# A graph layer and a mixture of experts on one core: nine chunks instead of eight, 33 stored blocks, and another listing of the accumulating transfers

## What is computed

```python
def gnn(features, src, dst, W, b):            # 6250 nodes, 106250 edges, 256 features
    xw = features @ W
    msg = xw[src] * rsqrt(max(out_degree, 1))[src][:, None]
    agg = segment_sum(msg, dst, 6250)
    return relu(agg * rsqrt(max(in_degree, 1))[:, None] + b)

def ffn(x):                                   # 8 experts, hidden width 1024, the 2 best for each row
    top_p, top_idx = top_k(softmax(x @ Wr + br), 2)
    weights = top_p / top_p.sum(-1)
    xe = layernorm(x) * ln_g[e] + ln_b[e]
    y[e] = gelu(xe @ W1[e] + b1[e]) @ W2[e] + b2[e]
    return weights[0] * y[top_idx[0]] + weights[1] * y[top_idx[1]]

x = x + gnn(layernorm(x), src, dst, W, b)
x = x + ffn(layernorm(x))
```

## Time and profile before

| | |
|---|---|
| device time, median of 3 runs (lowest, highest) | 1668.92 us (1660.3, 1669.75) |
| device time of the profiled execution | 1661.44 us |
| its span, first to last instruction | 1660.0 us |
| TensorE (PE) busy, weight loads (PEld) | 1192.6 us (72%), 989.6 us (60%) |
| VectorE (DVE), ScalarE (ACT), GpSimd (POOL) busy | 952.5 (57%), 595.0 (36%), 1116.0 us (67%) |
| mean granted TensorE clock | 0.82 |
| moved by DMA | 354.75 MB, mean 214 GB/s |

### The profile page before, as it was taken

One profiled execution on the slowest core, in us unless ns is written; L12 is line 12 of the kernel. 1 busy time (PEld: TensorE's weight loads), 2 busy tenths in 40 slices (PEclk: granted clock), 3 DMA queues, 4 the chain that ended last, 5 costly groups with the idle time before them and its releaser, 6 DMA issues.

```text
span 1660.0 us, 26618 instructions
## 1 busy us (share of the span) xinstructions
PE 1192.6 (72%) x9098; PEld 989.6 (60%) x9098; DVE 952.5 (57%) x2502; ACT 595.0 (36%) x1169; POOL 1116.0 (67%) x1115
## 2 busy tenths in 40 slices
PE   6954565647358645995599659969839858689995
PEld 5954344535146314982488439848728747479984
DVE  8997456656434353656264734764645749466552
ACT  4954011111032004440345025516315335356662
POOL 5006777777777777777777777777777757673333
PEclk9999566666578557996699769979959969799998
DMA  6027866675375447974787469759658578999882
GB/s 187 1 98 266 266 219 203 213 232 179 117 260 163 110 119 261 312 222 129 260 270 253 138 217 316 255 192 305 188 189 292 179 252 265 258 294 305 264 251 51
DMA packets 195546, 354.75 MB, mean 214 GB/s; under 512 B 25572, under 2 KB 93446, under 8 KB 195412
## 3 DMA queue, kind: packets, MB, share of 16 engines
q1 hardware_dynamic: 130120, 205.39, 36.6%
q0 software_dynamic: 58928, 141.26, 29.5%
q10 hardware_dynamic: 6364, 6.40, 1.2%
HBM read 290.80 MB, written 64.07 MB: 214 GB/s over the span
## 4 chain that ended last, share of the span: by engine, by line
PE 35%; DMA 25%; POOL 19%; issue 9%; DVE 8%; ACT 3%; SPq 0%; POOLq 0%; DVEq 0%; ACTq 0%
DMA gt<-zt,srcI 12%; POOL gt L832 9%; PE ps L1251 9%; PE ps L1266 9%; PE ps L1165 8%; DMA out<-gt,toks 6%; POOL xs L861 6%; DMA out<-acc 3%; PE ps L1140 2%; POOL out L891 2%; PE ps L1176 2%; DVE ohl L1340 2%; PE ps L1203 2%; DMA xb<-xs 1%; ACT h L1112 1%
## 5 line engine op out<-in xcount | busy, mean ns | idle before, releaser
L832 POOL DMA_INDIRECT gt<-zt,srcI x832 | 834.1, 1003 | 254.2 <-issue 181.6
L1165 PE MATMUL ps<-gt,S 128*128 128x257 f16 x1664 | 345.7, 331 | 200.3 <-DMA gt<-zt,srcI 198.9
L1165 PEld LDWEIGHTS ps<-gt,S 128*128 128x128 f16 x1664 | 203.5, 152 | 298.2 <-DMA gt<-zt,srcI 282.8
L1251 PE MATMUL ps<-xe,w1b 128*128 128x256 f16 x2688 | 343.2, 282 | 36.0 <-DVE xe L1656 18.9
L1266 PE MATMUL ps<-w2b,hT 128*128 128x256 f16 x2688 | 315.5, 275 | 13.5 <-DVE yb L1688 7.7
L1251 PEld LDWEIGHTS ps<-xe,w1b 128*128 128x128 f16 x2688 | 269.9, 101 | 78.6 <-DVE xe L1656 21.6
L1112 ACT ACTIVATE h<-ps,cb 128x256 f32<-128x256 f32 x448 | 227.1, 557 | 241.4 <-PE ps L1251 236.4
L1662 DVE SCALAR_TENSOR_TENSOR hT<-h,cb,hT 128x512 f16<-128x512 f32 x224 | 167.7, 750 | 237.4 <-ACT hT L1116 236.8
L1266 PEld LDWEIGHTS ps<-w2b,hT 128*128 128x128 f16 x2688 | 264.3, 99 | 47.5 <-issue 15.4
L1116 ACT ACTIVATE hT<-h,cb 128x512 f16<-128x512 f32 x224 | 161.7, 722 | 7.3
L1090 ACT ACTIVATE aT<-ps 128x256 f32<-128x256 f32 x98 | 37.4, 381 | 314.7 <-PE ps L1196 314.6
(11 more groups left out here) (264 smaller groups left out, 1246.7 us busy)
## 6 DMA issues: line engine op xcount, KB each, us to landing
w1b<-ws SPq DMA_DIRECT2D x56, 1024.0 KB, 6.5
w2b<-ws SPq DMA_DIRECT2D x56, 1024.0 KB, 8.1
ws<-w2b SPq DMA_DIRECT2D x16, 1024.0 KB, 5.0
xb<-xs SPq DMA_DIRECT2D x56, 260.0 KB, 8.3
gt<-zt,srcI POOLq DMA_INDIRECT x832, 4.2
ys<-yb SPq DMA_DIRECT2D x34, 256.0 KB, 7.8
w1b<-in_L_ffn_W SPq DMA_DIRECT2D x8, 1024.0 KB, 8.7
hT<-in_L_ffn_W SPq DMA_DIRECT2D x8, 1024.0 KB, 13.9
```

The source lines that it names most:

```text
L832: e.indirect_dma_start(out=gt[:, i % NG, :], out_offset=None, in_=zt, in_offset=bass.IndirectOffsetOnAxis(ap=srcI[:, c, r:r + 1].bitcast(u ...
L1165: inst = e.matmul(PS[r % 2][:, 0:257], S[:, r % NS, :, c], gt[:, i % NG, part * 257:part * 257 + 257], start=(c == 0 and part == 0), stop= ...
L1251: inst = e.matmul(UP[n % 2][:, z * BS:(z + 1) * BS], w[:, l, kk, j * 128:(j + 1) * 128], xe[m % 2][:, k, kk, :], start=(kk == 0 and l == 0 ...
```

## The change

`ENDS` gives nine chunks: the tiles behind 36 are cut at 40, 43, 46 and 49, not at 41, 45 and 49. The number of blocks in them goes from 5, 4, 18 to 4, 3, 3, 17. `EARLY` is counted from the end, so 33 blocks are stored and 23 given, and 40 tiles are fetched and combined. The sums go from three ranges (tiles 10 to 20, 20 to 30, 30 to 41) to two of 15 tiles. The groups behind tile 36 are complete after rows 86, 93, 99 and 104, where they were after 82, 89, 97 and 104.

In the planner a give or a sum is listed only when GpSimd will be free within 0.5 us, not 2.6; a give counts as 3.7 us of GpSimd and 4.5 until it has landed (3.4 and 5.0 before), a sum as 2.0 and 3.0 + 1.1 us a tile (1.3 us a tile of GpSimd and 5.0 before). A `cg` or `xs` step is listed only when GpSimd will be free within 0.3 us, and not when an accumulating transfer is waiting to be listed and the one before will have landed within the next microsecond; before, `cg` needed GpSimd free within 2.5 us and `xs` nothing. A `cc` comes 6 us behind its `cg` in the plan, not 2.

```diff
-ENDS = [10, 17, 24, 31, 36, 41, 45, 49]
+ENDS = [10, 17, 24, 31, 36, 40, 43, 46, 49]
...
-EARLY = LAST - 2
+EARLY = LAST - 3
...
-NSUM = -(-(TG - TP) // 11)
+NSUM = 2
...
     def step_give():
 
-        if max(s["chain"], s["plain"], s["base"]) > s["now"] or clock["POOL"] > s["now"] + 2.6:
+        if max(s["chain"], s["plain"], s["base"]) > s["now"] or clock["POOL"] > s["now"] + 0.5:
             return False
         if batches and batches[0][0] <= s["now"]:
             b = batches.popleft()[1]
-            emit("sums", b, (("POOL", 1.3 * (SUMS[b][1] - SUMS[b][0])),), s["now"])
+            emit("sums", b, (("POOL", 2.0),), s["now"])
+            s["chain"] = clock["POOL"] + 3.0 + 1.1 * (SUMS[b][1] - SUMS[b][0])
             s["summed"] += 1
         elif gives:
-            emit("give", gives.popleft(), (("POOL", 3.4),), s["now"])
+            emit("give", gives.popleft(), (("POOL", 3.7),), s["now"])
+            s["chain"] = clock["POOL"] + 4.5
             s["given"] += 1
         else:
             return False
-        s["chain"] = clock["POOL"] + 5.0
         return True
...
-                if kind == "cg" and clock["POOL"] > s["now"] + 2.5:
+                if kind in ("cg", "xs") and (clock["POOL"] > s["now"] + 0.3 or (gives or batches) and s["now"] + 1.0 < max(s["chain"], s["plain"], s["base"]) + 1.0 < s["now"] + 2.0):
                     continue
...
-                chain.at = end + 2.0 if kind == "cg" else s["now"] if kind == "xs" else end
+                chain.at = end + 6.0 if kind == "cg" else s["now"] if kind == "xs" else end
```

## The result

The changed kernel takes 1672.55 us (median of 8 runs, 1670.07 to 1674.4), the kernel before 1666.21 us in the runs beside it (8 runs, 1660.3 to 1670.04). The ratio is 1.0051, 95% interval 1.0035 to 1.0068: the change makes the kernel 0.5% slower, where 1641 us was forecast. In the profiled executions the span goes from 1660.0 to 1670.3 us.

What follows compares the result with a forecast made beforehand. No engine bounds the whole: first GpSimd's gathers, at the end the chain of accumulating transfers. First give 1390, plus 102.3 and 43, puts the twelfth give at 1535, the last at 1621, span 1631.7, median 1641; range 1624 to 1664.

Steps and rivals of the forecast that it cites:

- Fetch stage: GpSimd's gathers up to the last one: 43 tiles scattered before it, not 45, and first `cg` at 1338 to 1340.
- the 5.2 us: Before the last gather on GpSimd: 4 scatter DMAs of 1.30 us less, so it comes 5.2 us earlier.
- First give: First accumulating transfer after ten stored tiles: 1339 + 45.7 + 7.8, less stalls, taken as 1390, bounds 1385 and 1396.
- the old 45.7 us: Old time between first `cg` and first give, kept as base, with 7.8 us added for six scatters.
- Up to 4: Listing `cc` 6 us behind its `cg`, not 2, delays the tenth `cc` by up to 4 us.
- Sums: Two accumulating sums of 15 tiles in the chain: 21.5 us each, 43 together, bounds 29 and 48; three old ones took 47.3.
- the old 1.53 us a tile: Proportional cost of a sum from the old kernel: 1.53 x 15 = 22.9 us for fifteen tiles.
- Spacing of the gives: Gives while `cg` are still issued: two pairs behind each, 9.3 us apart, bounds 8.9 and 11.7, about 11 gives.
- the spacing stays: Rival: gives land late behind moving gathers, spacing near 11.7 us; span 1649, median 1658; chance 0.14.
- The last chunk and the late end: Last chunk's scatters at 1386, first `y` 1430, last 1606; final gives then at 5.5 us, last starting at 1621.
- The rival "slower": GpSimd runs behind its list, VectorE and TensorE wait, 5.9 us in each of 12 cycles; median 1693; chance 0.09.

Runs made afterwards that it cites:

- The chunks alone: Kernel before with the nine new chunks, old planner and three sums of ten tiles: 1675.43 us, ratio 1.0058.
- the planner's half alone: Changed kernel with the old chunks put back, new planner and two sums of 15 and 16 tiles kept: 1670.48 us, ratio 1.0022.
- the one-tile sum: Changed kernel with each of the two sums cut to its first tile, order of steps kept: 1657.66 us, ratio 0.9937.
- The loose listing: Changed kernel with only the conditions for listing a give, `cg` and scatter set back to the old ones: 1684.08 us, ratio 1.0112.
- The run that halved it by another order: Changed kernel with each `cc` gathered behind a sum listed only after that sum's planned landing: 1677.21 us, ratio 1.0061.

## Why the prediction was wrong, by its steps

The starts below are those of the forecast and of the changed kernel's trace.

| point | forecast | measured | lost up to here |
|---|---|---|---|
| first `cg` | 1339 | 1342.64 | 4 |
| last chunk's scatters | 1386 | 1391.77 | |
| first give | 1390 | 1413.47 | 23.5 |
| first give behind the last sum | 1498 | 1541.09 | 43.0 |
| last give | 1621 | 1660.45 | 39.5 |
| span | 1631.7 | 1670.3 | 38.6 |
| first, last `y` of the last chunk | 1430, 1606 | 1451.98, 1642.73 | 22, 36.7 |

The forecast did not say where the last sum stands. The fourth line is worked out from its terms for the seven gives that came before it: 1390 + 7 x 9.3 + 2 x 21.5 = 1498.1.

**Fetch stage, 4 us.** Before the last gather 43 tiles were scattered, as forecast, and the hole of 11.19 us in front of the first `cg` shrank to 4.48. But the four scatters fewer did not bring the 5.2 us: the last gather is issued at 1337.21, in the kernel before at 1336.81. The 832 gathers kept GpSimd busy 839.0 us, not 834.1; why is open.

**First give, 23.5 us: the failed step.** It was put as the old 45.7 us plus six scatters minus a few us of stalls. From the first `cg` to the first give it took 70.8 us (1342.64 to 1413.47), not 51. Its parts counted GpSimd's instructions, but the first give can't be issued before the tenth `cc` and its store, and that `cc` stands in VectorE's queue. The sentence "one routing more costs VectorE some 12 us of small instructions, in a stretch where it is busy 18.23 us of 40: nothing" took its cover from 1200:1240. In the stretch that mattered VectorE was already busy 44.53 us of 60 in the kernel before:

```profile
1340.00:1400.00 60.00, 50.52 (x390) 41.52 (x390) 44.53 (x142) 32.33 (x60) 38.15 (x38) 0.86 0.79 254
```

and is busy 47.91 of 60 after. That is only 3.4 us more, so the load alone doesn't explain 18 us: what matters is the order in the queue. The last chunk's routing, which came behind the tenth `cc`, now stands ahead of it. The tenth `cc` slips from 1383.34 to 1401.32. The chunks alone show it (1397.20), and listing it first gives 1385.51. The give then waits for a plain store too, 11.13 us in that run, for which the forecast had no term. And while the `cc` is late, the planner lists other work: 21 `cg` pairs and both chunks' twelve scatters go before the first give, where the forecast had 17 pairs and six scatters. It put the last chunk's scatters at 1386, ahead of its own first give, and had no term for them. "Up to 4" for the 6 us behind `cg` was small for the old chunks, where the planner's half alone delays the first give by 11.8 us.

**Sums, 9.0 us.** 26.75 + 25.23 = 52.0 us, not 43, outside the upper bound of 48, and more than the 45.9 that the old 1.53 us a tile make of 30 tiles. What was overlooked stands in the forecast's own rows: the DMA share was 1.02 from 1495 to 1510, so a sum's duration says what else was moving as much as what it moves itself. The runs bear that out: sums of ten tiles landed after 11.0 to 19.4 us, sums of fifteen after 18.2 to 27.5. There is a fixed part: one tile alone held the chain 8.23 us and each further tile added 1.2. By that line ten tiles would hold it 8.23 + 9 x 1.2 = 19.0 us; the last ten-tile sums with the new chunks held it 19.61 and 19.66, where the old kernel had 15.94 and 13.07. The first sum is another matter: with the 16 gathers listed behind it GpSimd was busy 23.0 us (21.8 with the one-tile sum), so with this list a shorter transfer could not bring it below that. The wrong step was to take durations of one stretch as those of another: the old kernel with two sums shows 21.82 and 25.76 us too, nothing less than its three.

The Trainium skill (DMA: Bandwidth & Descriptors, section on the anatomy of one DMA) gives 2.0 us plus bytes over 436 GB/s, by which 1.97 MB are an estimate of 6.5 us; the trace has 25.81 and 24.38. The measurement decides, and the formula holds here even less than for ten tiles.

**Spacing of the gives.** Four gives in front of the first sum take 36.99 us, where 4 x 9.3 = 37.2 was forecast: this step was right for these four, two pairs behind each give and no rival "the spacing stays". The loose listing shows 11.5 to 11.9 in its place. But there were seven gives in this phase and not eleven, since 21 pairs had gone ahead of the first give and not 17. And the three gives behind the first sum take 15.76, 11.55 and 11.34 us, 38.65 and not 27.9: 10.8 us. Behind a long sum the gathers and the give itself land late. The mean of 9.3 came from stretches with short sums.

The Trainium skill (same page, section on two DMAs through the same engine) says that descriptors of one queue start in order; the gathers issued behind the sum, with their 16.7 to 22.3 us, agree with it, and so do the 5.2 us behind the one-tile sum. What it doesn't tell is why the give at 1479.15 still takes 12.73 us, when the sum has landed. In the stretch from 1480 the DMA engines are full at half the bytes:

```profile
1480.00:1495.00 15.00, 15.00 (x122) 12.76 (x120) 11.88 (x32) 8.29 (x15) 6.66 (x7) 0.87 1.00 136
```

This stays open.

**The last chunk and the late end, 36.7 us at the last `y`.** From the last chunk's scatters to its first `y` 60.2 us passed, not 45.6. The three blocks of chunk 7 were to fit in between; their scatters went at 1352.63 and not near 1338. From the first instruction of their last group (1299.94) to their slots (1350.41) it took 50.5 us, where the four-tile chunk of the kernel before took 41.6 (1270.65 to 1312.29). Blocks 34 and 35, for which the forecast had no time here, had their `y` at 1351.04 and 1362.07. The last `y` of chunk 7 came at 1425.63, so TensorE was not free for the last chunk before. The forecast's 42 us for the last chunk's own routing was right (1342.86 to 1385.85, 43.0). Then the stand of 18.46 us fell into the last chunk. The forecast let the last `y` come at 1606, so that the last gives would go in a quiet tail at 5.5 us; the tail came, but 37 us later, and the 15 spacings behind the last sum took 119.4 us, not 122.8.

**The rival "slower".** Its mechanism is the nearest to what the trace shows: VectorE stands at a `cc` for late rows, and TensorE with it. Its price was wrong. It was not one of 5.9 us in each of twelve cycles, but stands of 5.80, 5.00 and 18.46 us, of which the long one is behind the sum. What the long one costs is known only roughly: without it, and without most of the sums' bytes, the last `y` came 5.8 us earlier. The run that halved it by another order brought other waits and can't tell.

**Where the expected gain went.** By the forecast the change was to win 28 us of span. The tighter gives won some 10 us (the loose listing is 0.6% slower), where the forecast's price for eleven of them was 26. The chunks took more than that at the first give, 18.4 us; the 6 us behind `cg` may have taken 4 us (0.24%, not clear of noise); and the sums held the chain 52.0 us where 43 were forecast (47.3 before). These parts are not additive, as nearly the same edits give other signs with the other chunks: the tight listing costs 0.45% there, two sums 0.25%.

**What stays open.** Undoing most of the late first give won 10.9 us there and 2.7 at the last give; the chain behind it took 8 us more. A part is plain. Gives cost 8.6 us beside weight loads and 5.5 in the quiet tail, which starts when TensorE ends. An advance moves gives out of the tail, and 5.5/8.6 = 0.64 of it is kept; an end of TensorE that comes later costs the other 0.36 of its delay. These are estimates: 0.64 x 10.9 = 7.0 us won, 0.36 x 6.0 = 2.2 lost by the later last `y`, 4.8 left. So some 2 us are unexplained, and no run shows an earlier first give without the delay of the last chunk. In the same way 22 us less of sums would be worth 14, between the 7.9 and the 19 us measured. Whether the DMA engines' total work, which no order of transfers shortens, sets a bound of its own was not measured by itself.

## What to carry to other kernels

Before transfers are packed more tightly or joined, read the DMA share of that stretch. Where it was 1.0 here, two long sums held the chain as long as three shorter ones in one kernel (47.6 and 47.3 us) and 5.7 us less in the other, and small transfers issued behind a long one from the same engine landed late. A step's cover has to be read in the very stretch in which the step will lie, and in the order of the queue in which the next thing stands; here that was VectorE's, with the tenth `cc` behind a routing. An advance in a chain of transfers that ends in a quiet tail is worth only the ratio of a quiet link to a busy one (0.64 here, an estimate), and less when the same edit makes the tail start later.

## What was unexpected of the hardware

Gathers of 128 rows issued behind an accumulating transfer of 15 tiles from the same engine landed after 16.7 to 22.3 us (median) in the changed kernel. The same gathers behind one of a single tile took 5.2 to 6.1. It varies: in the run with `cc` 2 us behind `cg`, behind 15 tiles that landed after 18.2 us, they took 6.2 to 12.4. Accumulating transfers of 1.97 MB took 18.2 to 27.5 us beside other traffic in these runs, those of 1.31 MB 11.0 to 19.4. And the same program took 1664 to 1668 us on some chips and 1939 and 1945 us on two others; why was not found.
